# A two-layer local-attention block on one core: one exponential for a pair of heads, keys and queries normalized before the turn, new written-out orders for every engine, and 381 instead of 161 products of constants

## The reference, cut to what matters

```python
def _layer(x, wqkv, qs, ksc, wo, lg, lb, w1, b1, w2, b2):
    q, k, v = split(shift_token(x) @ wqkv)          # 8 heads of 64
    q = l2norm(q) * qs
    k = l2norm(k) * ksc
    q, k = rotary_xpos(q, k)
    sim = einsum('bhwid,bhwjd->bhwij', q * QK_SCALE, look_around(k))   # windows of 64, with the one before
    sim = where(mask, -max, sim)
    attn = softmax(sim)
    x = x + (attn @ look_around(v)) @ wo
    h = layernorm(shift_token(x)) * lg + lb
    a, g = split(h @ w1 + b1)
    return x + (a * gelu(g)) @ w2 + b2
```

## Time and profile before

| what | value |
|---|---|
| three runs | 2141.57, 2145.38, 2145.68 us; median 2145.38 |
| the profiled execution | span 2140.7 us from first to last instruction, 4.7 us (0.2%) under the median of the runs |
| TensorE busy | 1949.1 us, 91% |
| TensorE weight load busy | 1117.7 us, 52% |
| ScalarE busy | 1607.3 us, 75% |
| VectorE busy | 1559.3 us, 73% |
| GpSimd busy | 862.1 us, 40% |
| mean granted TensorE clock | 0.989 of full speed |

### The profile page before, as it was taken

One profiled execution on the slowest core, in us unless ns is written; L12 is line 12 of the kernel. 1 busy time (PEld: TensorE's weight loads), 2 busy tenths in 40 slices (PEclk: granted clock), 3 DMA queues, 4 the chain that ended last, 5 costly groups with the idle time before them and its releaser, 6 DMA issues.

```text
span 2140.7 us, 56185 instructions
## 1 busy us (share of the span) xinstructions
PE 1949.1 (91%) x22308; PEld 1117.7 (52%) x22308; DVE 1559.3 (73%) x2671; ACT 1607.3 (75%) x3975; POOL 862.1 (40%) x826
## 2 busy tenths in 40 slices
PE   6789999999999999999999999999999999999987
PEld 3344545555454655545555554655545455554644
DVE  3476787877778777787877778687777877777753
ACT  1567878787887878777787887878688787877755
POOL 2043616245351624526163361625435162452522
PEclk8999999999999999999999999999999999999999
DMA  4110201213030120202112030120203012030100
GB/s 137 29 32 16 61 7 36 41 24 58 7 68 9 39 43 24 58 7 57 21 32 51 24 58 7 38 39 24 58 7 70 13 36 42 24 53 7 36 6 23
DMA packets 63110, 76.19 MB, mean 36 GB/s; under 512 B 10630, under 2 KB 57856, under 8 KB 60800
## 3 DMA queue, kind: packets, MB, share of 16 engines
q1 hardware_dynamic: 62852, 72.60, 16.1%
HBM read 9.14 MB, written 4.19 MB: 6 GB/s over the span
## 4 chain that ended last, share of the span: by engine, by line
PE 56%; ACT 23%; DVE 12%; issue 5%; SPq 2%; DMA 1%; POOL 1%; DVEq 0%; ACTq 0%; POOLq 0%
PE ps L430 10%; ACT pr L815 6%; PE ps L667 5%; PE ps L564 5%; ACT pr L777 5%; PE ps L594 4%; PE ps L595 4%; PE ps L604 4%; PE ps L658 3%; PE ps L449 3%; ACT pr L788 3%; DVE wm L1000 3%; PE ps L678 2%; PE ps L445 2%; PE ps L687 2%
## 5 line engine op out<-in xcount | busy, mean ns | idle before, releaser
L1091 POOL TENSOR_TENSOR pr<-pr 128x1024 f32<-128x1024 f32 x128 | 302.2, 2361 | 739.7 <-DVE pr L989 739.7
L815 ACT ACTIVATE pr<-ps,wb,inv 128x128 f32<-128x128 f32 x768 | 340.8, 481 | 24.6 <-DVE wb L1006 24.2
L777 ACT ACTIVATE pr<-ps 128x1024 f32<-128x1024 f32 x320 | 314.4, 1028 | 42.5 <-PE ps L449 42.0
L1108 POOL TENSOR_TENSOR pr<-pr,shares 128x512 f32<-128x512 f32 x192 | 199.9, 1048 | 314.0 <-DVE shares L1021 314.0
L947 DVE TENSOR_REDUCE nm<-ps 128x2 f32<-128x256 f32 (+2 forms) x384 | 314.5, 861 | 13.0 <-PE ps L449 11.9
L430 PE MATMUL ps<-cf,pr 128*128 128x128 f32 x1792 | 259.7, 282 | 31.1 <-POOL pr L1108 22.5
L430 PEld LDWEIGHTS ps<-cf,pr 128*128 128x128 f32 x1792 | 200.9, 142 | 124.4 <-issue 55.0
L982 DVE TENSOR_TENSOR pr<-ps,rot 128x1024 f32<-128x1024 f32 x128 | 156.2, 1221 | 120.1 <-ACT pr L788 97.7
L788 ACT ACTIVATE pr<-ps 128x1024 f32<-128x1024 f32 x128 | 131.2, 1025 | 104.6 <-PE ps L595 66.2
L445 PE MATMUL ps<-cb 64*64 64x256 bf16 (+1 forms) x2560 | 175.3, 263 | 30.1 <-ACT pr L777 14.4
L1014 DVE COPY pr<-ps 128x512 f32<-128x512 f32 x256 | 170.1, 679 | 15.2 <-PE ps L430 13.7
(11 more groups left out here) (158 smaller groups left out, 4040.0 us busy)
## 6 DMA issues: line engine op xcount, KB each, us to landing
pr<-V SPq DMA_DIRECT2D x32, 512.0 KB, 4.5
queries<-early SPq DMA_DIRECT2D x224, 64.0 KB
keys<-early SPq DMA_DIRECT2D x224, 64.0 KB
pr<-V SPq DMA_DIRECT2D x32, 384.0 KB, 6.6
xn<-in_L_attn_x SPq DMA_DIRECT2D x16, 256.0 KB, 4.5
out<-hT SPq DMA_DIRECT2D x16, 256.0 KB, 2.2
queries<-mT SPq DMA_DIRECT2D x128, 4.0 KB
Wqkv<-in_L_ffn_wqkv SPq DMA_DIRECT2D x1, 1536.0 KB
```

The lines of the kernel that those rows point to most:

```text
L777: act.activation(dst, src, ACT.Exp, scale=SC1).then_inc(ex_r[s], 1)
L815: ins = act.activation(P2[s][2 * (p % 3) + r][:, o:o + P], bank[:, r * T + o:r * T + o + P], ACT.Exp, scale=inv[s][:, t, h:h + 1], bias=wb ...
L1091: pool.tensor_tensor(t1[s][t % 3], t1[s][t % 3], t2[s], ALU.add).then_inc(sum_r[s], 1)
L1108: pool.tensor_tensor(part, part, share, ALU.mult).then_inc(part_r[s], 1)
```

## The change

1. **Softmax.** The queries are normalized by GpSimd before the turn, as the keys were. The scores need no scale then: VectorE takes the maxima (1037), adds the negated maxima to the whole pair of heads and writes it to SBUF (1042), which frees the two banks. ScalarE makes one exponential of 128 x 1024 without a side result (848). VectorE adds up the rows (1051) and inverts them (1055). The multiplication of the maxima by the inverse norms is gone.
2. **Copies.** The turned shares are copied out of PSUM by ScalarE (855), no longer by VectorE.
3. **qkv by halves.** Queries and keys take a bank each, and squares, cosines, sines and the addition are done for each half by itself.
4. **Orders.** PLACES, TURNS and FIRST_BANKS are new. Even and odd sequences have orders of their own, so that what repeats is two sequences long.
5. **Products of constants.** 381 in place of 161: in the middle 28 for two sequences (14 for one), where there were 5 for one.

The core of the diff (the tables are cut to a line, since their numbers tell a reader nothing):

```diff
 FILLS = {
-    2: 2, 7: 20, 17: 7, 69: 10, 70: 3, 74: 2, 77: 6, 103: 1, 187: 4, 188: 1, 332: 4, 333: 1, 477: 4, 478: 1, 622: 4,
...
+    7: 20, 15: 1, 31: 1, 45: 4, 46: 1, 53: 3, 60: 7, 63: 2, 68: 10, 69: 3, 75: 10, 83: 9, 87: 11, 88: 1, 94: 2,
...
@@ TensorE, qkv
-                        bank, full = banks.take(pe, (b, "qkv", l, t), [t_r.at(b, 3 * n)], 2)
+                        bank, full = banks.take(pe, (b, "qkv", l, t, j), [t_r.at(b, 3 * (2 * (n - 1) + j + 1))])
@@ TensorE, wscore
-                        bank, full = banks.take(pe, (b, "wscore", l, p), [we_r.at(b, 2 * n + 2)], 2)
+                        bank, full = banks.take(pe, (b, "wscore", l, p), [wd_r.at(b, n + 1)], 2)
@@ ScalarE
                     elif kind == "wexp":
+                        l, p = a
+                        act.wait_ge(*wd_r.at(b, NP2 * l + p + 1))
+                        act.activation(P2[s][p % 3], P2[s][p % 3], ACT.Exp).then_inc(we_r[s], 1)
+                    elif kind == "pturn":
                         l, p, r = a
...
-                        for t in range(NT):
-                            o, h = t * P, 2 * p + r
-                            ins = act.activation(P2[s][2 * (p % 3) + r][:, o:o + P], bank[:, r * T + o:r * T + o + P], ACT.Exp,
-                                                 scale=inv[s][:, t, h:h + 1], bias=wb2[s][:, t, h:h + 1],
-                                                 accum_out=sums[s][:, t, h:h + 1])
-                        ins.then_inc(we_r[s], 1)
...
+                        act.activation(PT[s][:, (2 * n + r) % 3, :], bank, ACT.Copy).then_inc(pt_r[s], 1)
@@ VectorE, wscore
-                        dve.tensor_tensor(wb2[s][:, :, 2 * p:2 * p + 2], wm2[s][:, :, 2 * p:2 * p + 2],
-                                          inv[s][:, :, 2 * p:2 * p + 2], ALU.mult).then_inc(wb_r[s], 1)
...
+                        dve.tensor_tensor(P2[s][p % 3].rearrange("p (j n) -> p j n", n=P), src.rearrange("p (j n) -> p j n", n=P),
+                                          low.unsqueeze(2).broadcast_to([P, 2 * NT, P]), ALU.add).then_inc(wd_r[s], 1)
@@ VectorE, share
-                        dve.reciprocal(shares[s][:, :, h], sums[s][:, :, h]).then_inc(share_r[s], 1)
...
+                        dve.tensor_reduce(total, P2[s][p % 3].rearrange("p (j n) -> p j n", n=P), AX_X, ALU.add).then_inc(sum_w[s], 1)
...
+                        dve.reciprocal(shares[s][:, 2 * p:2 * p + 2, :].rearrange("p r t -> p (r t)"), total).then_inc(share_r[s], 1)
@@ GpSimd, norm
-                        v = t1[s][t % 3][:, T:2 * T].rearrange("p (h d) -> p h d", d=D2)
-                        one = inv[s][:, t, H2:2 * H2].unsqueeze(2).broadcast_to([P, H2, D2])
-                        pool.tensor_tensor(v, v, one, ALU.mult).then_inc(rot_r[s], 1)
+                        for j in range(2):
+                            v = t1[s][t % 3][:, j * T:(j + 1) * T].rearrange("p (h d) -> p h d", d=D2)
+                            one = inv[s][:, t, j * H2:(j + 1) * H2].unsqueeze(2).broadcast_to([P, H2, D2])
+                            pool.tensor_tensor(v, v, one, ALU.mult).then_inc(rot_r[s], 1)
```

More of the change, by code:

```diff
@@ L141 @@
+    "SP": (
+        "02bd20d7d20d7d20d7d20d7d20d7d20d7d20d7db"),
 }
 def merged(engine):
-    names = [steps()[i] for i in PLACES[engine]]
-    rest = [iter([(b, name) for k in range(B // S2 + 1) for back, name in names for b in [s + S2 * (k - back)] if 0 <= b < B])
-            for s in range(S2)]
+    names = steps()
+    rest = [iter([(b, names[i % len(names)]) for k in range(B // S2 + 4) for i in PLACES[engine][s]
+                  for b in [s + S2 * (k - i // len(names))] if 0 <= b < B]) for s in range(S2)]
@@ L328, in build @@
         ctx2 = [a[:, 0:4 * T].rearrange("p (h n) -> p h n", n=T) for a in scr]
-        sums = [sb(f"sums{s}", [P, NT, H2]) for s in range(S2)]
-        shares = [sb(f"shares{s}", [P, NT, H2]) for s in range(S2)]
+        sums = [sb(f"sums{s}", [P, H2, NT]) for s in range(S2)]
+        shares = [sb(f"shares{s}", [P, H2, NT]) for s in range(S2)]
         hid = [a[:, 0:3 * T].rearrange("p (c n) -> p c n", n=T) for a in scr]
```

265 lines of the change are left out of this document (139 added, 126 removed), and 68 rows, old and new, of tables (FILLS, PLACES).

## The result

The changed kernel takes 2163.2 us (median of four runs, 2161.8 to 2166.0), the kernel before 2144.5 on the same chip: 1.0087 of it, with an interval of 1.0073 to 1.0102. It is 0.87% slower; the forecast was 2130 and faster. The profiled execution has a span of 2160.0 us against 2140.7, 19.3 more.

A forecast was written before the change was run, and what follows sets the result against it. TensorE was taken to bound the kernel; waits per period of 3.9 + 3.4 + 1.7 = 9.0 us against 9.8 win 11 us in fourteen periods, the ends 4: span 2126, median 2130, range 2085 to 2168.

The forecast's parts named there:

- TensorE is the bound, and ScalarE's gain is not the period's: Whole period: TensorE, busy 118.3 of 126.7 us, sets the time; only its waits can be won, though ScalarE loses 10 us.
- The rule of matmul busy time: Whole period: by weight-load time TensorE has 68.1 of 126.7 us, so ScalarE's 10 us would come off each, giving 2005.
- The loads of the other engines: Busy time per period: ScalarE 100.4 to 90.3 us, VectorE 96.7 to 105, GpSimd from 54 to 61.
- Place A: Second layer's softmax: TensorE's waits and constants of 3.8 us a period become waits of 3.9, so +0.1.
- Place B: Second MLP and first softmax: TensorE's waits of 2.2 us a period become 3.4, so +1.2.
- I take these three waits as gone and 0.4 of the small ones, 3.8 becomes 1.7: Rest of the period: two first-attention exponential waits (0.9), others of 0.4 and 0.4 us vanish or shrink, -2.1 a period.
- no wait by the sum, but no cover either: Between A and B: GpSimd's last keys ready at 43.2 us, TensorE at their turn at 43 as well.
- The rival of a late GpSimd: Turns between A and B: GpSimd 2 to 3 us late, period +1.4, +20 us, 2165; chance 0.17.
- the rival of a longer place B: Second MLP and first softmax: waits of 5.5 us instead of 3.4, period 128.0, +18 us, 2163; chance 0.11.
- Its products are the same. Without the five constants it works 116.9 us: TensorE's own work per period: unchanged products, 116.9 us without constants, leaving 9.8 us of waits or constants.
- The ends: First and last sequences: 4 us won by the clock at the end, 4 at the start, 4 given back; -4 in all.
- the +4 for the longer chain of a lone sequence: At the ends: 4 us given back because a lone sequence's chain gains four multiplications of queries.

## Why the prediction was wrong

The forecast was a span of 2126 us, the trace has 2160. In the fourteen periods 11 us were to be won and 11.8 were lost; at the ends 4 were to be won and 7.5 were lost.

**TensorE is the bound, and ScalarE's gain is not the period's: right.** ScalarE came down by 11.0 us a sequence and the period rose. The rule of matmul busy time (the Trainium skill, Perfetto Trace Analysis, Identifying the Most-Contended Engine) would have made 2005 of it. The measured 2163.2 us do not agree.

**The loads of the other engines: right** to 2 us, as said above. One term lay outside its bounds: an addition by halves on GpSimd was to take 1.05 to 1.18 us and took 1.27.

```profile
L1126 POOL TENSOR_TENSOR pr<-pr 128x512 f32<-128x512 f32 x256 | 321.7, 1274 | 594.8 <-DVE pr L1025 594.8
```

**Place A, forecast 3.9 us: right.** Constants counted from start to start, the even side has 1.66 + 1.02 + 0.64 + 0.20 + 0.33 = 3.9 (forecast 3.5), the odd one 1.73 + 1.55 of constants + 0.51 + 0.17 = 4.0 (4.2). The forecast's terms for VectorE add up to 12.0 us and not 12.2, which changes little.

**Place B, forecast 3.4: right in the sum, less so in the parts.** The even side has 0.85 ahead of it, then 1.65 of constants and 0.69, 3.2 (forecast 3.8), the odd one 0.78 + 0.17 + 1.91 and 0.58 of constants, 3.4 (3.2). The waits ahead are 0.8 where the sum had 0.25, those behind are shorter than it had them. On the odd side TensorE waits for the copies behind four table loads, as the forecast said, and the run with the exponential moved shows that it hangs on the loads: without two of them 1.7 us come back there. The Trainium skill, page ScalarE: Activation LUTs, section What ACT_TABLE_LOAD costs, adds a drain of 1.38 us to a load. The trace does not agree: the copies of 1286.53 start 0.02 us behind the end of the load of 1285.23.

**"I take these three waits as gone and 0.4 of the small ones, 3.8 becomes 1.7": too low.** Waits and constants are 6.0 + 3.4 = 9.4 us a sequence (9.0 forecast, 9.8 before), so 2.2 is left for the rest. 0.4 of it is GpSimd's.

Forecast and trace are thus 1.9 us a sequence apart (-0.8 and +1.1): 0.4 in waits and constants, 1.5 in what TensorE is busy with. Two steps of the prediction failed there.

**GpSimd, "no wait by the sum, but no cover either": the first step that failed, 0.8 of the 1.9 us.** Leaving the queries' product out gives back 0.8 us a sequence: 0.4 that the profile lists as waits for line 1137, and 0.4 that had looked like TensorE's work. The sum had the last keys and TensorE at the turns both at 43 us. It took six additions at 1.18 us; at the 1.27 measured they alone make the keys 0.5 us late, and the lateness here is 0.86 us on the even side and 0.64 on the odd one. The rival of a late GpSimd, given 0.17, had the place and the mechanism right and the size wrong: it priced 2 to 3 us of lateness. That its 2165 is near the measured 2163 is luck; so is the 2163 of the rival of a longer place B, which was not longer.

**"Its products are the same. Without the five constants it works 116.9 us": the second step that failed, the other 1.1 us.** Without constants (3.4 us, from start to start) TensorE works 121.8 - 3.4 = 118.4 us a sequence, 1.5 more, of which GpSimd's share is 0.4. Products are the same in number, but not in what they stand beside: the order has 60 changes a sequence between products on the whole array and on a part of it, where it had 54. Counted from start to start in six sequences of each trace, the listed waits taken off, 21 of a sequence's whole f32 passes over 512 columns stood beside a part product before and took 2.1 us more than 429 ns each; after, 29 took 2.9 more: 0.8 us. The part products themselves (scores and maxima of both attentions) took 25.9 us against 25.2, 0.7 more. The other whole passes took 0.5 more, of which 0.3 are gone without the queries' product, and all other products 0.4 less. The extra constants show that such a side has a price of its own. That the sides are all of the 1.1 is argued and not shown: no run here has the new orders with the old number of sides, idle time under 0.15 us is not listed as a wait, and the queries' product shows that such waits exist.

**The ends, forecast -4 us: wrong, +7.5.** Start 2.6 later, last sequence 4.9 longer. What the forecast expected of the clock came: the mean granted clock rose from 0.95 to 0.96 ahead of the first addition and from 0.93 to 0.98 behind the fifteenth, and without the constants there the kernel is 13.6 us slower. So the term that failed is the +4 for the longer chain of a lone sequence; it was 7.5 or more. In the last sequence TensorE's constants wait 3.4 us for VectorE's sines and 1.8 for ScalarE's copies of the keys, where before the longest such wait was 4.2, for ScalarE's copies of the queries. Which part of the 4.9 is which step's was not tried; without the queries' product it is 80.0, so it isn't that one. The 2.6 of the start is near the 1.8 by which two traces with the same start differ.

No version here beats the kernel before.

## What to carry to other kernels

"The same products" is a term to be priced, not a zero: ask for each moved product whether its neighbours fill the same part of the array (0.1 us a side here), and count these sides in the order. A gain at one wait is only kept if the clock is; look at the granted clock in the stretch behind it before and after. A small new step on an idle engine (here 47% busy) is as expensive as its place in a back-to-back chain: four tiles at 5.0 us with no gap were all it took, and half of what it cost looked like TensorE's work. And a run that comes out the same can be a gain and a loss: look at each place before calling a step free.

## What was not expected of the hardware

- Constants cost nothing where they were put and 0.09, 0.21 or 0.32 us each elsewhere, for the same 0.21 us product. Among part products one moves the next start by 0.42 us.
- Without the 196 between the ends the clock falls in stretches of 3.4 us in six of seven pairs of sequences, in a kernel whose TensorE is busy 91% of the time. At one place the same wait of 1.9 us had such a stretch in two pairs of the changed kernel and in five of the run with one product on VectorE.
- A bf16 product over 64 x 64 of the array holds it longer than one over 128 x 128 with as many columns, 0.33 against 0.23 us, when a whole f32 product stands behind it.
